# A transformer layer in fp32: how softmax weights meet the latents, and where their sums and the rounding constants are made

## The reference

```python
xn = layernorm(x)                                   # 16 x 512 x 256, eps 1e-5
# attention, 8 heads of 64, latent rank 64
q = xn @ Wq.T ; lat = xn @ Wkv_down.T
k = lat @ Wk_up.T ; v = lat @ Wv_up.T
attn = softmax(q @ k.T * 64 ** -0.5)                # per head, 512 x 512
y1 = (attn @ v) @ Wo.T
# feed-forward, inner width 704
def fq(a): scale = max(max|block of 16| / 6, 1e-12); return grid(a / scale) * scale   # 0, .5, 1, 1.5, 2, 3, 4, 6
h = silu(fq(xn) @ fq(w_gate).T) * (fq(xn) @ fq(w_up).T)
y2 = fq(h) @ fq(w_down).T
out = x + y1 + y2
```

## Time and profile before

| | |
|---|---|
| median of 3 runs | 1718.05 us (1705.89 to 1718.47) |
| profiled execution | 1717.89 us, its span 1716.0 us |
| busy share: TensorE, its weight loads, VectorE, ScalarE, GpSimd | 93%, 84%, 78%, 41%, 30% |
| DMA | 4% of 16 engines, 13 GB/s |
| mean granted TensorE clock | 0.969 of full |
| costliest groups | L909 (P x latents): 4096 products, 519.5 us busy, their loads 523.8; row maxima L616: 512 of 682 ns; exp L511: 512 of 595 ns |

### The profile page before, as it was taken

One profiled execution on the slowest core, in us unless ns is written; L12 is line 12 of the kernel. 1 busy time (PEld: TensorE's weight loads), 2 busy tenths in 40 slices (PEclk: granted clock), 3 DMA queues, 4 the chain that ended last, 5 costly groups with the idle time before them and its releaser, 6 DMA issues.

```text
span 1716.0 us, 33440 instructions
## 1 busy us (share of the span) xinstructions
PE 1589.8 (93%) x10726; PEld 1449.4 (84%) x10726; DVE 1342.3 (78%) x3368; ACT 709.0 (41%) x1382; POOL 518.9 (30%) x696
## 2 busy tenths in 40 slices
PE   1599999999999999999999999899998999999998
PEld 0488988989889898888989899898988989899897
DVE  7788887878878787788768878778887878887664
ACT  2444443443434443444443444344443444344432
POOL 7433232233323232232323323222323223222211
PEclk9799999999999999999999999999999999999999
DMA  3000000000000000000000000000000000000000
GB/s 97 10 7 4 14 14 7 17 8 20 4 10 20 5 20 7 12 14 8 17 9 20 4 14 13 6 20 7 10 14 10 17 7 20 4 14 8 1 14 13
DMA packets 22932, 23.11 MB, mean 13 GB/s; under 512 B 3280, under 2 KB 22224, under 8 KB 22736
## 3 DMA queue, kind: packets, MB, share of 16 engines
q1 hardware_dynamic: 22736, 20.65, 4.0%
...
## 4 chain that ended last, share of the span: by engine, by line
PE 82%; DVE 11%; issue 5%; ACT 1%; DMA 0%; DVEq 0%; POOL 0%; SPq 0%; ACTq 0%; POOLq 0%
PE m L779 34%; PE po L909 22%; PE mx L868 7%; PE st L894 6%; PE st L895 6%; PE m L881 2%; PE m L1015 2%; PE m L933 1%; DVE row_max L616 1%; PE m L1021 1%; DVE hid L600 1%; DVE on_lo L750 1%; PE m L1029 1%; DVE h_small L588 1%; ACT q_hi L551 1%
## 5 line engine op out<-in xcount | busy, mean ns | idle before, releaser
L909 PEld LDWEIGHTS po<-lat_tok,probs 128*128 128x128 f32 x4096 | 523.8, 194 | 23.0 <-DVE on L685 0.3
L909 PE MATMUL po<-lat_tok,probs 128*128 128x65 f32 x4096 | 519.5, 271 | 0.0
L511 ACT ACTIVATE probs<-st 128x512 f32<-128x512 f32 x512 | 291.2, 595 | 339.0 <-PE st L895 339.0
L616 DVE TENSOR_REDUCE row_max<-mx 128x1 f32<-128x512 f32 x512 | 327.8, 682 | 0.7 <-PE mx L868 0.6
L416 POOL TENSOR_TENSOR h_norm<-hid,h_small 128x352 f32<-128x352 f32 x128 | 101.1, 790 | 481.9 <-DVE h_small L593 481.9
L894 PE MATMUL st<-q_hi,lat 128*128 128x512 f32 x512 | 212.7, 415 | 0.0
L895 PE MATMUL st<-q_lo,lat 65*128 65x512 f32 x512 | 203.6, 398 | 0.0
L779 PE MATMUL m<-wgu_hi,xt_hi 128*128 128x352 f32 x512 | 195.4, 382 | 8.6 <-issue 8.4
L447 POOL TENSOR_TENSOR h_norm<-h_norm,hid 128x352 f32<-128x352 f32 x128 | 119.8, 936 | 216.9 <-DVE h_norm L602 216.9
L868 PE MATMUL mx<-lat,q_hi 128*128 128x512 f32 x512 | 179.0, 431 | 4.0 <-DVE row_max L616 3.9
L729 DVE TENSOR_TENSOR q_lo<-m,q_hi 64x512 fp32r<-64x512 f32 x128 | 88.1, 688 | 120.6 <-ACT q_hi L551 120.6
...
## 6 DMA issues: line engine op xcount, KB each, us to landing
x_in<-in_L_attn_x_dram SPq DMA_DIRECT2D x64, 128.0 KB, 2.1
...
q_lo<-neg_max SPq DMA_DIRECT2D x128, 2.0 KB
...
```

Source lines behind the costliest of these rows:

```text
L511: act.activation(probs[:, t.c % 2, kc, :], st[kc % 2][:, :], ACT.Exp).then_inc(exp_done, 1)
L616: dve.tensor_reduce(row_max[:, u.c % 2, qc:qc + 1], mx[qc % 2][:, :], AX.X, ALU.max).then_inc(mx_taken, 1)
L909: last = pe.matmul(po[:, qc * P:qc * P + R + 1], probs[:, u.c % 2, kc, qc * P:(qc + 1) * P], lat_tok[:, s.c % 2, kc, 0:R + 1], start=(kc = ...
```

## The change

P x latents changes sides: 64 columns of `lat_tok` are the stationary operand and P is streamed, 512 queries at a time. The two heads of a pair go to PSUM partitions 0 to 63 and 64 to 127 of bank `po`, and to the two halves of the array's columns. The result comes out as (head, latent) x queries, so the transposes of `on` go away. All of a pair's P x latents, 8 fp32 matmuls, stands at the start of the even slot after the pair (`weigh(t)`), and is followed there by the row sums: GpSimd adds the four key chunks of P (`add_keys`, three additions a head) into `key_sum`, and 16 fp32 matmuls with 64 columns of `key_sum` (every eighth query) as the stationary operand and one column of ones as the streamed one put the sums into bank `m2`, 128 partitions x 8. VectorE takes the reciprocal; a DMA writes them to DRAM and two more read them back, each head's 512 values to 64 partitions (`inv_b`). VectorE scales the pair in one step in the odd slot, ScalarE copies `on_hi` at the start of the next slot and GpSimd subtracts `on_lo`. The output projection moves one slot back, and the tail has one slot more. Of the rounding, ScalarE makes the constants of h and x by square and copy, as for the weights, ahead of the queries' copies (h) and behind them (x); VectorE keeps the addition, which moves to the end of its slot.

Not shown: declarations of semaphores, and the same `w_set` on the new shape of `on`.

```diff
-        on = sb("on", [P, 2, CH, P])
+        on = sb("on", [P, T])
+        inv_b = sb("inv_b", [P, T])
+        key_sum = sb("key_sum", [P, 2, T])
+        h_magic = sb("h_magic", [P, HALF], BF16)
+        x_magic = sb("x_magic", [P, D], BF16)
-        inv_den = sb("inv_den", [P, 2, CH])
+        inv_den = sb("inv_den", [P, 2, T // R])
+        inv_rows = nc.dram_tensor("inv_rows", (2, 2, T), F32).ap()
...
@@ -261,19 +274,28 @@
-        def turned_pair(t):
+        def weighed_pair(t):
...
+        def scaled_pair(t):
+
+            m = t.plus(-3).over(2)
+            return m if t.c % 2 and m.within(B * PAIRS) else None
+
+        def split_pair(t):
+
+            return weighed_pair(t.plus(-2))
...
             s = t.over(H).plus(-1)
-            m = s.times(2, t.c % H - 1)
-            return m if t.c % H in (1, 2) and m.within(B * 2) else None
+            m = s.times(2, t.c % H - 2)
+            return m if t.c % H in (2, 3) and m.within(B * 2) else None
         LEAD = [At(c) for c in range(-12, 0)]
-        TAIL = [At(SLOTS + c) for c in range(4)]
+        TAIL = [At(SLOTS + c) for c in range(5)]
@@ -375,10 +397,21 @@
+                m = weighed_pair(t)
+                if m is not None:
+
+                    sp.wait_ge(inv_done, m.n(1, 1))
+                    sp.dma_start(inv_rows[m.c % 2].rearrange("v (p j) -> (v p) j", p=R), inv_den[:, m.c % 2, :]).then_inc(inv_stored, 16)
...
+
+                if m is not None:
+                    sp.wait_ge(inv_stored, m.n(16, 16))
+                    for v in range(2):
+                        sp.dma_start(inv_b[v * R:(v + 1) * R, :],
+                                     inv_rows[m.c % 2, v:v + 1, :].broadcast_to([R, T])).then_inc(inv_spread, 16)
@@ -437,23 +470,44 @@
+            def add_keys(t, kc):
+
+                total, last = key_sum[:, t.c % 2, :], probs[:, t.c % 2, kc, :]
+                pool.wait_ge(exp_done, t.n(CH, kc + 1))
+                if kc == 1:
+                    if t.over(2).any():
+                        pool.wait_ge(den_psum, t.over(2).n())
+                    first = probs[:, t.c % 2, 0, :]
+                else:
+                    pool.wait_ge(sum_step, t.n(CH - 1, kc - 1))
+                    first = total
+                pool.tensor_tensor(total, first, last, ALU.add).then_inc(sum_step, 1)
...
-
-                    pool.wait_ge(h_round, w.n(ROUND_STEPS, ROUND_STEPS))
+                    add_keys(w, 3)
+                m = split_pair(t)
+                if m is not None:
+
+                    pool.wait_ge(on_hi_done, m.n(1, 1))
+                    pool.tensor_tensor(on_lo[:, m.c % PAIRS, :], on[:, :], on_hi[:, m.c % PAIRS, :].bitcast(F32),
+                                       ALU.subtract).then_inc(on_lo_done, 1)
+                if w.within(SLOTS):
+
+                    pool.wait_ge(h_round, w.n(1, 1))
...
                         pool.wait_ge(ht_psum, w.n(1, -1))
-                    pool.tensor_tensor(h_norm[:, :], h_norm[:, :], hid[:, w.c % 2, :], ALU.subtract).then_inc(h_grid, 1)
+                    pool.tensor_tensor(h_norm[:, :], h_norm[:, :], h_magic[:, :], ALU.subtract).then_inc(h_grid, 1)
...
-                    pool.wait_ge(x_round, n.n(ROUND_STEPS, ROUND_STEPS))
+                    pool.wait_ge(x_round, n.n(1, 1))
...
                         pool.wait_ge(xt_psum, n.n(1, -1))
-                    pool.tensor_tensor(x_norm[:, :], x_norm[:, :], xq[:, n.c % 2, :], ALU.subtract).then_inc(x_grid, 1)
+                    pool.tensor_tensor(x_norm[:, :], x_norm[:, :], x_magic[:, :], ALU.subtract).then_inc(x_grid, 1)
@@ -478,6 +532,9 @@
                     weights(t, 1)
+                if t.within(SLOTS):
+                    add_keys(t, 1)
+                    add_keys(t, 2)
@@ -506,16 +563,26 @@
-                        if t.any(CH, kc + 1 - 2 * CH):
-                            act.wait_ge(pv_done, t.n(CH, kc + 1 - 2 * CH))
+                        if t.over(2).any(CH, kc + 1 - CH):
+                            act.wait_ge(pv_done, t.over(2).n(CH, kc + 1 - CH))
+                        if kc == 0 and t.any(CH - 1, 1 - CH):
+                            act.wait_ge(sum_step, t.n(CH - 1, 1 - CH))
...
+                m = split_pair(t)
+                if m is not None:
+
+                    act.wait_ge(on_done, m.n(1, 1))
+
+                    if m.over(PAIRS).any(2):
+                        act.wait_ge(wov_psum, m.over(PAIRS).n(2))
+                    act.activation(on_hi[:, m.c % PAIRS, :], on[:, :], ACT.Copy).then_inc(on_hi_done, 1)
...
                     if t.any(1, -1):
-                        act.wait_ge(h_grid, t.n(1, -1))
+                        act.wait_ge(h_norm_done, t.n(1, -1))
@@ -534,6 +601,11 @@
                 exp(3)
+                if t.within(SLOTS):
+                    act.wait_ge(h_norm_done, t.n(1, 1))
+                    act.activation(hid[:, t.c % 2, :], h_norm[:, :], ACT.Square, scale=MAGIC_SQUARE).then_inc(h_square, 1)
+                    act.wait_ge(h_square, t.n(1, 1))
+                    act.activation(h_magic[:, :], hid[:, t.c % 2, :], ACT.Copy, bias=MAGIC_LEAST).then_inc(h_magic_done, 1)
@@ -550,20 +622,18 @@
                                            ACT.Copy).then_inc(q_hi_done, 1)
+                n = norm_chunk(t)
+                if n is not None:
+                    act.wait_ge(x_norm_done, n.n(1, 1))
+                    act.activation(xq[:, n.c % 2, :], x_norm[:, :], ACT.Square, scale=MAGIC_SQUARE).then_inc(x_square, 1)
+                    act.wait_ge(x_square, n.n(1, 1))
+                    act.activation(x_magic[:, :], xq[:, n.c % 2, :], ACT.Copy, bias=MAGIC_LEAST).then_inc(x_magic_done, 1)
...
                                    ACT.Copy).then_inc(xt_hi_done, 1)
-                m = turned_pair(t)
-                if m is not None:
-
-                    act.wait_ge(on_psum, m.n(1, 1))
-
-                    if m.over(PAIRS).any(2):
-                        act.wait_ge(wov_psum, m.over(PAIRS).n(2))
-                    act.activation(on_hi[:, m.c % PAIRS, :], m2[:, :], ACT.Copy).then_inc(on_hi_done, 1)
@@ -634,6 +704,13 @@
             def slot(t):
+                m = weighed_pair(t)
+                if m is not None:
+
+                    dve.wait_ge(den_psum, m.n(1, 1))
+                    if m.any(1, -1):
+                        dve.wait_ge(inv_stored, m.n(16, -16))
+                    dve.reciprocal(inv_den[:, m.c % 2, :], m2[:, 0:T // R]).then_inc(inv_done, 1)
@@ -671,19 +748,15 @@
                     scales(h, h_small[:, t.c % 2, :, :], h_scales, t)
-                v = t.plus(-1)
-                if v.within(SLOTS):
-
-                    m, inv = v.over(2), inv_den[:, v.c % 2, :]
-                    heads = po[:, :].rearrange("p (c r) -> p c r", c=CH)
-                    dve.wait_ge(pv_done, v.n(CH, CH))
-                    dve.reciprocal(inv, heads[:, :, R]).then_inc(inv_done, 1)
-                    dve.wait_ge(inv_done, v.n(1, 1))
-
-                    if m.any(1, -1):
-                        dve.wait_ge(on_psum, m.n(1, -1))
-                    dve.tensor_tensor(on[:, m.c % 2, :, v.c % 2 * R:(v.c % 2 + 1) * R], heads[:, :, 0:R],
-                                      inv.unsqueeze(2).broadcast_to([P, CH, R]), ALU.mult).then_inc(on_done, 1)
+                m = scaled_pair(t)
+                if m is not None:
+
+                    dve.wait_ge(inv_spread, m.n(32, 32))
+                    dve.wait_ge(pv_done, m.n(CH, CH))
+                    if m.any():
+                        dve.wait_ge(on_hi_done, m.n())
+                        dve.wait_ge(on_lo_done, m.n())
+                    dve.tensor_tensor(on[:, :], po[:, :], inv_b[:, :], ALU.mult).then_inc(on_done, 1)
@@ -713,9 +786,6 @@
                     scales(xn[:, b, :], x_small[:, b, :, :], x_scales, n)
-                if t.within(SLOTS):
-                    dve.wait_ge(h_norm_done, t.n(1, 1))
-                    to_grid(h_norm[:, :], hid[:, t.c % 2, :], h_round, t)
@@ -744,20 +814,20 @@
                                       xt_hi[:, v, :, c * P:(c + 1) * P].bitcast(F32), ALU.subtract).then_inc(xt_lo_done, 1)
-                m = turned_pair(t)
-                if m is not None:
-                    dve.wait_ge(on_hi_done, m.n(1, 1))
-                    dve.tensor_tensor(on_lo[:, m.c % PAIRS, :], m2[:, :], on_hi[:, m.c % PAIRS, :].bitcast(F32),
-                                      ALU.subtract).then_inc(on_lo_done, 1)
...
                                       ALU.add).then_inc(ltok_done, 1)
+                if t.within(SLOTS):
+                    dve.wait_ge(h_norm_done, t.n(1, 1))
+                    dve.wait_ge(h_magic_done, t.n(1, 1))
+                    dve.tensor_tensor(h_norm[:, :], h_norm[:, :], h_magic[:, :], ALU.add).then_inc(h_round, 1)
...
                     dve.wait_ge(x_norm_done, n.n(1, 1))
-                    to_grid(x_norm[:, :], xq[:, n.c % 2, :], x_round, n)
+                    dve.wait_ge(x_magic_done, n.n(1, 1))
```

(64 more changed lines are left out.)

12 lines of the change are left out of this document (9 added, 3 removed).

## The result

The changed kernel took 1828.48 us (median of 4 runs, 1823.67 to 1833.29) against 1716.83 for the kernel before in the same comparison: ratio 1.068, 95% interval 1.062 to 1.075. The forecast was 1710.

What follows compares the result with a forecast made beforehand. TensorE was busy 93%; afterwards a loop of waits through all engines would set most pairs. A sequence: 101.3 us against 102.1; 16 of these -13, program end +6: -7, hence 1710 us, range 1620 to 1860.

Steps and rivals of the forecast that it cites:

- P x latents 3.63 us, overlapped: TensorE's 16 streamed instructions a pair: the two heads' column tiles run side by side, 3.63 us a pair.
- serial streams: Rival: the two heads' P x latents run one after another, 6.83 us a pair; 1855 us, chance 0.22.
- Denominators 1.7 us: TensorE's row sums: 32 loads of 64 strided columns a pair at 0.053 us each, 1.7 us; ends 0.85 and 3.4.
- dear loads: Rival: the denominators' strided loads cost 3.4 us a pair, moving their end back 1.7; 1820 us, chance 0.12.
- The loop, 24.3 us: Chain from one pair's denominators through TensorE, ScalarE, VectorE, GpSimd and xt_lo to the next denominators: 24.3 us.
- TensorE waits inside this: TensorE's waits within the loop: 0.4 us for ht_lo, about 1.5 before odd hidden transposes, about 1.5 before denominators.
- the other pairs at 24.3, 24.5 and 28.2: Forecast periods in us: pair with the latents 24.3, with the latents' transposes 24.5, with both projections 28.2.
- edits costed at nothing: VectorE's lost steps and changed meetings with GpSimd, and the reciprocals' DRAM trip, were not priced within the pairs.
- The clock: After 1.5 us TensorE stalls, the 1.2 GHz level may or may not come, about 3 us each time.
- Reciprocals by DRAM hidden: Two DMAs in a row, 2.1 us each, needed about 14 us after the denominators; bare only at program end.
- Constants on ScalarE: ScalarE's square and constant in the loop, 0.50 us each, ahead of four q_hi copies and xt_hi.
- The signs named: Expected in the trace: VectorE idle several us a pair before the reciprocal, TensorE waiting for xt_lo, GpSimd busy about 1090 us.

Runs made afterwards that it cites:

- e5: Changed kernel with P x latents ordered as head 0's four key chunks, then head 1's, so neighbours mostly share a column tile; 1852.6 us.
- e2: Changed kernel without GpSimd's additions of key chunks; the denominators read a tile of ones, so output is not normalised; 1750.4 us.
- e1: Changed kernel without VectorE's two additions of the rounding constants; a one-column memset with the same waits stands in their place; 1808.3 us.
- e20: e19 plus six more P x latents matmuls (12 instructions) in the pair whose denominators wait for xt_lo; 1817.8 us.
- e11b: Changed kernel with ScalarE's square and constant for x moved to the end of its slot, behind the lat_tok copy; 1827.4 us.
- e19: Changed kernel with the up product computed twice more ahead of TensorE's wait for lat_tok, as filler; 1833.7 us.
- e4: Kernel before the change, with only ScalarE's squares and rounding constants for h and x added; 1747.6 us, ratio 1.020.
- e3: Changed kernel with the rounding constants of h and x made on VectorE again; 1961.3 us, ratio 1.144.
- e17: Changed kernel without VectorE's two additions and their waits; GpSimd waits for ScalarE's constants itself; 1812.3 us.
- e8: Changed kernel with P x latents spread chunk by chunk over the even slot, denominators and reciprocal behind the fourth key score; 1793.8 us.
- e9: e8 with the even head's key sums moved into the odd slot on GpSimd; 1787.9 us.
- e15: Changed kernel with contiguous key sums, P x latents spread, even head's sums in the odd slot, additions behind row maxima, ScalarE's constants last; 1727.3 us.
- e16: e15 with VectorE scaling po behind the last row maxima; 1712.3 us, ratio 0.998.

## Why the prediction was wrong

- *P x latents 3.63 us, overlapped*: right (3.58). The rival "serial streams", 1855, did not happen. No gap shows where the tiled products begin (921.67) or where the denominators end (927.52).
- *Denominators 1.7 us*: 2.02 to 2.09. Half as much for overlap, twice for the stride; 0.3 to 0.4 us a pair, 20 to 25 us in all. That the sum was so near was luck. The total lies near the rival "dear loads" (1820), but not for its reason: that had 3.4.
- *The loop, 24.3 us*: right in the plain pair, step by step (24.7), and in the latents' pair once the additions are gone (24.5). Its GpSimd terms were right: 1.28 us a key sum for 1.27, 1081 us busy for 1090. e5 shows it as a loop: 1.3 us more of TensorE's work left the plain pair at 24.8. But e2 shows a second path of 23.8 us right behind it, so that the loop explains only the last 0.9 us.
- **The step that failed: "TensorE waits inside this", with waits of 0.4 and about 1.5 us inside the loop's slack, and the other pairs at 24.3, 24.5 and 28.2.** They took 26.4, 27.5 and 30.6: 7.5 us a sequence, where the 118 us missed are 7.4. Even in the plain pair the waits lay elsewhere: 0.3 us at the odd slot's hidden transposes, where the sum had 1.5, and 1.45 at the denominators. What counts in the other pairs is the path through VectorE's queue to the odd slot's row maxima, which the sum did not follow. In parts: in the latents' pair 1.9 us are VectorE's additions, stretched from 0.4 to 1.5 us beside GpSimd (e1), which "edits costed at nothing" names and does not price. In the pair with the projections 1.8 go when the wait ahead of the denominators of the plain pair is filled, and with it the half clock behind them (e20). In the pair with the latents' transposes 1.8 of the 3.0 go with the lat_tok wait (e11b), but the pairs after it give them back.
- *The clock*: I wrote that stalls of 1.5 us may or may not bring the lower level, and put it at zero in the sum. In the changed kernel the trace has it behind all three stalls, 13.6 us a sequence, at most 6.7 lost. The earlier trace rows had a price ready, 2.15 us of waiting and 6 us at 0.50. But "may or may not" was the right reading: in e5 waits of 1.50 and 1.98 us were followed by the full clock. e5 also bounds the cost. It added 86 us of work and took 24 more, so 62 came back; 24 of these are the wait for xt_lo that it filled. An estimate from these figures is 38 us for 148 us less at 0.50, where the clock's share alone gives 74. By the same reckoning e20 against e19 gives 16 + 41 - 20 = 37 us for 98 less, where the share gives 49. By these two estimates the slow clock cost between half and three quarters of the 6.7 us.
- *Reciprocals by DRAM hidden*: right; 1.4 and 2.9 us to landing, never waited for.
- *Constants on ScalarE*: the sum had them in its loop, at 1.0 us, and did not ask what they do alone. They cost 30 us where GpSimd makes no sums (e4) and are a gain of 133 where it does (e3).
- *The signs named*: TensorE's wait for xt_lo at the denominators came (24.0 us), and GpSimd's busy time; VectorE idled 1.6 us a pair ahead of the reciprocal (100.9 us in 64), not several.

What stays open is how the 7.5 us split in one sum. Taking out one wait moved it to another name and total times came out equal (e11b and the changed kernel, e17 and e1), so the parts above are not additive. What decides whether the clock falls behind a wait is not shown. That the four blocks were filler is argued from their return in e8, e9, e15 and e16, each time together with other edits; no run moves them alone.
